# The difference of a half tile begins after its sum: an ordering on GpSimd in a forward transform stage

## The reference, cut to what matters

```python
    x = x + _L0_conv_ref(_gn(x), ...)
    x = x + _L1_conv_ref(_gn(x), w1_real, w1_imag, w2_real, w2_imag)

    def _L1_conv_ref(x, w1_real, w1_imag, w2_real, w2_imag):
        x_ft = jnp.fft.rfft2(x)
        top = jnp.einsum('bixy,ioxy->boxy', x_ft[:, :, :m1, :m2], w1)
        bot = jnp.einsum('bixy,ioxy->boxy', x_ft[:, :, -m1:, :m2], w2)
        ...
        return jnp.fft.irfft2(out_ft, s=(h, w))
```

## Time and profile before

| what | value |
|---|---|
| median of 3 executions | 2686.02 us (2683.16 to 2687.36) |
| profiled execution | 2688.57 us, its span 2686.7 us |
| TensorE busy | 2148.0 us (80%) |
| VectorE busy | 2080.3 us (77%) |
| ScalarE busy | 1404.0 us (52%) |
| GpSimd busy | 935.1 us (35%) |
| mean rate of the DMA engines | 350 GB/s |
| median from issue to landing of a tile's load (1024 KB halves) | 8.6 us |

### The profile page before, as it was taken

One profiled execution on the slowest core, in us unless ns is written; L12 is line 12 of the kernel. 1 busy time (PEld: TensorE's weight loads), 2 busy tenths in 40 slices (PEclk: granted clock), 3 DMA queues, 4 the chain that ended last, 5 costly groups with the idle time before them and its releaser, 6 DMA issues.

```text
span 2686.7 us, 34793 instructions
## 1 busy us (share of the span) xinstructions
PE 2148.0 (80%) x12978; PEld 1220.7 (45%) x12978; DVE 2080.3 (77%) x2296; ACT 1404.0 (52%) x1757; POOL 935.1 (35%) x577
## 2 busy tenths in 40 slices
PE   0000089999999999999999999987777998988795
PEld 0000035665534664353555555567674554544452
DVE  7999979999999999999988888863324665545453
ACT  1111188898889888897777777741002221212110
POOL 2000024564335553366866656631101221111121
PEclk9999999999999999999999999998988999989897
DMA  9999789999999999998876777679998999999999
GB/s 399 431 430 422 333 266 345 340 347 344 341 340 349 335 343 339 338 348 313 318 258 255 258 263 266 260 281 346 367 382 331 416 416 417 416 418 417 417 417 384
DMA packets 404589, 940.99 MB, mean 350 GB/s; under 512 B 13868, under 2 KB 309084, under 8 KB 360780
## 3 DMA queue, kind: packets, MB, share of 16 engines
q1 hardware_dynamic: 213244, 577.01, 57.5%
q0 software_dynamic: 54672, 210.67, 20.0%
q10 hardware_dynamic: 136512, 151.14, 16.0%
HBM read 653.42 MB, written 285.08 MB: 349 GB/s over the span
## 4 chain that ended last, share of the span: by engine, by line
PE 49%; DMA 15%; DVE 12%; issue 7%; ACT 3%; POOL 1%; ACTq 0%; SPq 0%; DVEq 0%; POOLq 0%
PE psum L629 21%; DMA out<-arena 8%; PE psum L1119 8%; PE psum L998 7%; PE psum L1046 4%; PE psum L1093 4%; PE psum L1010 3%; DMA arena<-L_conv_w_imag 3%; DVE arena L1264 3%; DVE arena L896 2%; DVE arena L903 2%; DMA arena<-modes_out 2%; PE psum L1109 2%; DVE arena L1284 2%; ACT arena L643 1%
## 5 line engine op out<-in xcount | busy, mean ns | idle before, releaser
L629 PE MATMUL psum<-arena 128*64 128x512 f32 x4096 | 882.7, 592 | 2.2 <-DVE arena L732 1.8
L629 PEld LDWEIGHTS psum<-arena 128*64 128x64 f32 x4096 | 447.0, 136 | 437.7 <-issue 328.9
L1119 PE MATMUL psum<-tab_irow_icol,inv_t 128*128 128x512 f32 x1024 | 491.0, 603 | 46.7 <-ACT inv_t L1250 46.5
L1434 DVE TENSOR_TENSOR arena<-arena,psum 128x1024 f32<-128x1024 f32 x256 | 312.5, 1221 | 224.1 <-PE psum L1119 221.2
L1471 POOL TENSOR_TENSOR arena<-arena 128x1024 f32<-128x1024 f32 x128 | 347.9, 2726 | 191.7 <-PE psum L998 177.4
L534 POOL COPY arena<-arena 64x2321 f32<-64x2321 f32 x126 | 349.1, 2771 | 14.8 <-PE psum L629 7.1
L675 ACT ACTIVATE arena<-arena,pcur 128x2048 f32<-128x2048 f32 x128 | 268.1, 2095 | 106.4 <-DVE arena L903 101.8
L903 DVE SCALAR_TENSOR_TENSOR arena<-arena 128x2048 f32<-128x2048 f32 x128 | 319.2, 2494 | 4.0
L896 DVE SCALAR_TENSOR_TENSOR arena<-psum,pcur,arena 128x2048 f32<-128x2048 f32 x128 | 300.5, 2347 | 27.3 <-PE psum L629 26.7
L323 DVE BATCH_NORM_STATS2 arena<-arena 128x6 f32<-128x512 f32 x512 | 305.4, 676 | 14.2 <-DMA arena<-x 14.0
L1250 ACT ACTIVATE inv_t<-psum 128x256 f32<-128x256 f32 x256 | 97.5, 384 | 418.6 <-PE psum L1109 418.6
(11 more groups left out here) (192 smaller groups left out, 1823.9 us busy)
## 6 DMA issues: line engine op xcount, KB each, us to landing
arena<-x_scratch SPq DMA_DIRECT2D x254, 1024.0 KB, 8.6
arena<-x SPq DMA_DIRECT2D x120, 1280.0 KB, 9.4
arena<-x SPq DMA_DIRECT2D x64, 2048.0 KB, 12.4
x_scratch<-arena ACTq DMA_DIRECT2D x128, 1024.0 KB, 9.1
out<-arena POOLq DMA_DIRECT2D x126, 1024.0 KB, 41.6
arena<-L_conv_w_real POOLq DMA_DIRECT2D x6, 4096.0 KB, 19.8
arena<-L_conv_w_imag POOLq DMA_DIRECT2D x6, 4096.0 KB, 28.5
arena<-x SPq DMA_DIRECT2D x8, 1152.0 KB, 7.2
```

The lines of the kernel that those rows point to most:

```text
L629: last = nc.tensor.matmul(bank(k * 4 + q, 512, C, e * C), wcur[j][:, e, m * C:(m + 1) * C], taps[e][:, r0:r0 + 2, m:m + W], start=(m == 0) ...
L1119: last = nc.tensor.matmul(bank(n % 2 * 2 + a), TS[n % 2][:, a * P:(a + 1) * P], icol, start=True, stop=True)
L1434: nc.vector.tensor_tensor(xw, xw, psum[:, n % 2 * 1024:n % 2 * 1024 + 1024] .rearrange("p (a k) -> p a k", a=2), ALU.add).then_inc(added, 1)
```

## The change

GpSimd waits before each difference until the sum of the same half tile is done. Before, it did so only for half tiles 0 and 1, whose sums it computes itself. The semaphore `sums_done` counts the sums in order, on GpSimd for the first two and on VectorE from then on; no instruction that computes is added, removed or altered.

```diff
                         if h < 2:
                             nc.gpsimd.tensor_tensor(ED[h][0][:, :, :], XWF[0][:, 0, half, :], XWF[0][:, 1, half, :],
                                                     ALU.add).then_inc(sums_done, 1)
-                            pool.wait_ge(sums_done, h + 1)
+                        pool.wait_ge(sums_done, h + 1)
                         nc.gpsimd.tensor_tensor(ED[h % NE][1][:, :, :], XWF[t % NXF][:, 0, half, :],
                                                 XWF[t % NXF][:, 1, half, :], ALU.subtract).then_inc(diff_done, 1)
```

## The result

The changed kernel takes 2690.89 us (median of 20) against 2686.55 for the kernel before (20): ratio 1.0022, 95% interval 1.0014 to 1.0029, so some 6 us slower by the ratio (3.8 to 7.8) and 4.3 by the medians. The forecast was 2687, within 0.2%, in a range of 2677 to 2701. The time lies in the range; but the likeliest case was a difference too small to tell from nothing, and what came is a small loss, the second likeliest.

What follows compares the result with a forecast made beforehand. No engine is full over the span; in the forward stage, sums and differences block each other. Start +3.4, six images -7.2, end +3.9 and weights +1 sum to +1.1 us: 2687 on the median 2686.02, range 2677 to 2701.

Steps and rivals of the forecast that it cites:

- What bounds the stage, the blocking inside records: Forward stage: VectorE sums and GpSimd differences take turns, each waiting inside its own record; 3.33 us per half tile without columns.
- the rival of the short chain: Forward stage: hand-over 0.03, difference 2.24, sum 1.09 give 3.47 us a step; 2675, or as likely 2681; chance 0.22.
- The chain of 3.67 us a step: Forward stage outside columns: row start, sum, hand-over, difference, hand-over take 7.33 us over two half tiles, 3.67 each.
- (a): Stretch with column products: 9.36 us a pair exceeds the chain's 7.33, so the later difference is hidden, 2.0 us in hand.
- (b): One image: 67.75 us against 68.95, mean addition and spread no longer held up; -1.2 an image, -7.2 for six.
- The rival in which the difference takes the memory before the tiny instructions: Mean addition and spread still wait behind a difference, 1.2 us each, seven times: 2704, or 2696 for one; chance 0.12.
- (c): Start of the forward stage: steps of 3.67 us put the first columns at 1321.5 instead of 1318.1; +3.4 us.
- U(6): Start of TensorE's row products of half tile 6 in the first image, forecast at 1274.5 us.
- F: Start of the first column products of all, from the span's start; forecast at 1321.5 us.
- (d): End of the forward stage: two weight transfers, some 2.9 us, issued before difference 127 now delay it; +3.9 us.
- (e): Weights issued 7.0 us later, mostly absorbed by 6 nearly empty us of the DMA engines; +1, bounds 0 and +7.
- The rival of +7: Mixing stage is bound by its transfers, so the weights' delay passes on whole: +7 instead of +1, 2693; chance 0.10.

Runs made afterwards that it cites:

- tiny_only: Kernel before, with only two differences an image waiting, one for the addition of the mean, one for the spread, none for its sum; 2654.63 us, ratio 0.9882.
- mean_only: Kernel before, with only the wait of one difference an image (half tiles 32, 48, ... 112) for the addition of the mean; 2674.55 us, ratio 0.9959.
- spread_only: Kernel before, with only the wait of one difference an image (half tiles 20, 36, ... 116) for the spread; 2668.09 us, ratio 0.9934.
- weights_last: Changed kernel, with the first weight transfers issued after the last difference (127) instead of before it; 2697.05 us, ratio 1.0041.
- tail_free: Changed kernel, but from half tile 122 on the difference doesn't wait for its sum; 2690.24 us, ratio 1.0011.
- weights_124: Changed kernel, with the first weight transfers issued before difference 124 instead of before 127; 2689.59 us, ratio 1.0014.

## Why the prediction was right or wrong, point by point

- *What bounds the stage, the blocking inside records:* right. Sums and differences at 1.22 and 2.37 us, the tiny instructions at 0.21 and 0.14. The difference of 2.24 us, on which the rival of the short chain rested, isn't found: behind a sum that is done it takes 2.37.
- *The chain of 3.67 us a step:* right, 3.69. The hand-overs that no row had shown are 0.17 (taken: 0.15) and 0.10 (taken: 0.05).
- *(a) Columns:* right, 9.36 us a pair in every kernel.
- *(b) An image:* 67.89 against 67.75, six images -6.4 against -7.2. That the gain comes from the tiny instructions is borne out by tiny_only, mean_only and spread_only. The rival in which the difference takes the memory before the tiny instructions is out: both go first.
- *(c) The start:* the course of the changed kernel was right (U(6) and F come out within 0.5 us of 1274.5 and 1321.5, counted from L1336), the base it was set against was not typical. +3.4 was the distance to one profile of the kernel before, whose rows at 1313.50 ran at the lower clock. That the measured pair gives +3.7 is in part luck: against profiles with the same number of falls it is +5.8 to +6.3, by F over all profiles +5.5.
- *(d) The end:* mis-sized. The last difference is late by 3.9 us as worked out (55.4 from the columns to the last rows), but the rows behind the stall ran at the lower clock, and the end came 5.5 us later. The same fall of the clock stood in the earlier trace rows and was not carried over.
- *(e) The weights:* the step whose reasoning failed. It took +1 because the DMA engines had 6 empty us. These lie 96 us behind image seven's first columns, and the first chunk starts at 77.9: they come too late for what is held up, the first modes, which stand behind the weights. The cost is 2.7 us at the first chunk. The rival of +7 was right that the empty us don't absorb the delay; but of the 10.7 us by which the weights are late only 2.7 are paid beyond the later end of the half tiles, so in size +1 was nearer. Measured for (d) and (e) together: +8.0 at the third chunk against 4.9.

The sum by the profiles is 5.5 - 6.4 + 8.0 = +7 us. Counted to the end of the span, the changed kernel takes 6.1 us more from image seven's first columns on and not 8.0 (961.0 against 954.9), which gives 5.5 - 6.4 + 6.1 = +5; the ratio says +5.9, against +1.1 predicted. The forecast was thus off by about 5 us, by some 2 in (c), 1 in (b) and the rest in (d) and (e), all to the same side. The time still lies in the range, but the range was drawn for steps between 3.47 and 3.88 us, and the step came as forecast; that it also held the errors of the other terms was not planned.

Open is why the clock fell in some profiles of the same stall and not in others, and how often it does so over many executions.

## What to carry to other kernels

When two engines block each other, what matters is whom a queued instruction stands in front of: here two VectorE instructions of 0.14 and 0.20 us cost 28 us in six images ((68.95 - 64.22) x 6), because a GpSimd instruction of 2.4 us was queued each time. Holding back just that one instruction, by a wait on the tiny one's semaphore, gives 1.2%; putting the engines in order everywhere ends the same blocking but puts both durations into one chain and makes all that is queued behind them late. Before ordering a queue, look at what it issues at its end: here the issue of two transfers came to stand in front of the last difference (with it moved behind, in weights_last, the last spread came 3.0 us sooner), and the late transfers held up the modes behind them (2.7 us). And before trusting one profile as a base, see at which clock its rows ran: one fall was worth 2 us here, where the whole change was worth 6.

## What the runs showed of the hardware

- A 64x1 addition on VectorE took 2.32 us beside a GpSimd difference (4.20 in tail_free, where differences ran from half tile 122 on without a wait) and 0.14 without it.
- VectorE's next instruction starts before GpSimd can: 0.09 us before the sum's end as recorded against 0.17 after it (1429.76 + 1.22, 1430.89, 1431.15).
- Behind a stall of 2.65 us TensorE's rows ran at the lower clock in two of four profiles (3.63 and 3.35 us against 1.94). One such fall put the first columns 2.0 to 2.4 us later.
- A transfer of the modes asked for at the same moment landed 9.6 us after its issue with the weights issued early (weights_124) and 18.1 us after it with the weights 11 us later (changed kernel).
